# Graph network kernel: layout of the 32-bit one-hots in the bounded attention path

## The reference, cut to what matters

```python
hp = einsum('nf,hfo->hno', h, w)
e = leaky_relu(a_src[:, src] + a_dst[:, dst] + fc_b, 0.2)      # a score of each edge and head
e = exp(e - segment_max(e, src))
att = e / segment_sum(e, src)
out = mean over heads of segment_sum(att * hp[:, dst], src) + bias
```

## Time and profile before

| | |
|---|---|
| three runs | 20199.39, 20180.35, 20198.07 us; median 20198.07 us |
| profiled execution | 20195.53 us, of which its span is 20193.8 us |
| busy over the span | PE 12823.5, PEld 10964.2, DVE 14189.8, ACT 8582.0, POOL 10831.2 us |
| pairs of the attention stage | first exponent at 8914.3 us, last at 10463.8 us of the span |
| `widen_hots`, L2521 | 440 instructions, 2023 to 2157 ns each |
| mean granted TensorE clock | 0.741 of full over the span |

### The profile page before, as it was taken

One profiled execution on the slowest core, in us unless ns is written; L12 is line 12 of the kernel. 1 busy time (PEld: TensorE's weight loads), 2 busy tenths in 40 slices (PEclk: granted clock), 3 DMA queues, 4 the chain that ended last, 5 costly groups with the idle time before them and its releaser, 6 DMA issues. The chain is left out here.

```text
span 20193.8 us, 373564 instructions
## 1 busy us (share of the span) xinstructions
PE 12823.5 (64%) x81513; PEld 10964.2 (54%) x81515; DVE 14189.8 (70%) x35200; ACT 8582.0 (42%) x18845; POOL 10831.2 (54%) x11458
## 2 busy tenths in 40 slices
PE   1333333334444444459985888888878888888887
PEld 1333333334444444448873555555567777777776
DVE  5187773113222222248877999899989999999999
ACT  5611112221000000039964777577745555555554
POOL 2777777775777777741111000000037777777776
PEclk8555555555555555569987999999988888888988
DMA  2212122224322233235532333223322222222223
GB/s 65 17 16 15 15 15 17 17 17 52 69 69 68 69 69 69 69 49 49 49 34 81 102 102 102 86 102 102 103 55 43 43 43 43 43 43 43 43 43 40
DMA packets 2940092, 1096.13 MB, mean 54 GB/s; under 512 B 2414118, under 2 KB 2633479, under 8 KB 2938505
## 3 DMA queue, kind: packets, MB, share of 16 engines
q1 hardware_dynamic: 2510328, 650.25, 17.0%
q0 software_dynamic: 312576, 231.97, 7.2%
q10 hardware_dynamic: 117044, 212.38, 3.7%
HBM read 999.36 MB, written 98.48 MB: 54 GB/s over the span
## 5 line engine op out<-in xcount | busy, mean ns | idle before, releaser
L2782 POOL DMA_INDIRECT conv_far<-conv_rows x3232 | 3065.9, 949 | 2922.0 <-DMA att_far_all<-rows_by_src 2072.9
L818 POOL DMA_INDIRECT weighted_far<-in_x_dram,weighted_rows x3232 | 3338.2, 1033 | 1295.3 <-issue 984.9
L1557 POOL DMA_INDIRECT rows_by_src<-push_row,push_index x3232 | 3103.5, 960 | 1004.8 <-issue 984.9
L908 PE MATMUL weighted_total<-weighted_message,weighted_hot 128*128 128x33 f32 x6464 | 1542.9, 404 | 2817.9 <-ACT weighted_message L932 2686.4
L1334 DVE TENSOR_SCALAR hop_hots<-hop_wide_iota,hop_nodes 128x512 bf16<-128x512 f16 x11904 | 3306.2, 384 | 2.1 <-PE hop_sums_ps L1407 2.1
L2888 PE MATMUL conv_radial_a<-radial,conv_hidden 128*128 128x256 f32 x6464 | 2741.9, 512 | 637.8 <-DVE conv_products_b L3020 570.5
L1407 PE MATMUL hop_sums_ps<-hop_hots,place_i 128*96 128x512 bf16 x11904 | 2827.2, 380 | 494.3 <-DVE hop_hots L1334 376.4
L1633 PE MATMUL push_near<-far_rows_sb,push_turned 128*128 x6464 | 1682.3, 434 | 2123.4 <-DVE push_turned L1596 2122.8
L908 PEld LDWEIGHTS weighted_total<-weighted_message,weighted_hot 128*128 128x128 f32 x6464 | 1438.8, 328 | 2922.7 <-issue 2922.2
L1633 PEld LDWEIGHTS push_near<-far_rows_sb,push_turned 128*128 128x128 f32 x6464 | 1569.5, 327 | 2186.7 <-issue 2186.4
L2888 PEld LDWEIGHTS conv_radial_a<-radial,conv_hidden 128*128 128x128 f32 x6464 | 1802.8, 327 | 701.2 <-issue 636.6
(11 more groups left out here) (349 smaller groups left out, 23978.7 us busy)
## 6 DMA issues: line engine op xcount, KB each, us to landing
hop_line<-sources_of_tiles SPq DMA_DIRECT2D x744, 512.0 KB
push_line<-local_by_group ACTq DMA_DIRECT2D x808, 256.0 KB
conv_weights<-weight_by_group SPq DMA_DIRECT2D x808, 128.0 KB
att_far_all<-rows_by_src SPq DMA_DIRECT2D x880, 80.0 KB
weighted_rows<-edges_by_dst SPq DMA_DIRECT2D x3232, 4.0 KB
weighted_far<-in_x_dram,weighted_rows POOLq DMA_INDIRECT x3232, 2.4
push_place<-place_by_dst SPq DMA_DIRECT2D x3232, 0.5 KB
rows_by_src<-push_row,push_index POOLq DMA_INDIRECT x3232
```

The lines of the kernel that those rows point to most:

```text
L818: pool.indirect_dma_start(far[s][:, j, :], None, table, bass.IndirectOffsetOnAxis(ap=rows[s][:, j, 0:1].bitcast(I32), axis=0)).then_inc(ga ...
L908: last = pe.matmul(total[:].rearrange("p n c -> p (n c)")[:, bass.ds(at[s % SLOTS * HALVES + j // COLUMNS], width)], hot[b][:, j, :], mess ...
L1557: pool.indirect_dma_start(k.rows_by_src, bass.IndirectOffsetOnAxis(ap=index[s][:, j:j + 1], axis=0), row[s][:, j, :], None).then_inc(writt ...
L2782: pool.indirect_dma_start(far[s][:, j, :], None, k.conv_dram, bass.IndirectOffsetOnAxis(ap=rows[s][:, j, 0:1].bitcast(I32), axis=0)).then_ ...
```

## The change

`hot_pair(q)` keeps its place and size. A new view of it, `wide_hot(q)`, has the node outermost and the tile innermost, [128 nodes, 8 tiles], the order of `short_hot`. ACT writes through it, now reading and writing in one piece. PE takes the weights of a tile from it with a step of eight 32-bit values.

```diff
+        def wide_hot(q):
+            return hot_pair(q).rearrange("p g j n -> p (g j n)").rearrange("p (n c) -> p n c", c=2 * PER)
...
-                        last = pe.matmul(part[q % 2][:, g * HEADS * W:(g + 1) * HEADS * W], hot_pair(q)[:, g, j, :],
-                                         message_pair(q)[:, g * PER + j, :], start=(j == 0), stop=(j == PER - 1))
+                        last = pe.matmul(part[q % 2][:, g * HEADS * W:(g + 1) * HEADS * W],
+                                         wide_hot(q)[:, :, g * PER + j], message_pair(q)[:, g * PER + j, :], start=(j == 0), stop=(j == PER - 1))
...
-                act.copy(hot_pair(q).rearrange("p g j n -> p (g j) n"),
-                         short_hot[q % 2][:].rearrange("p n c -> p c n")).then_inc(p_hot_widened[q % 2], 1)
+                act.copy(wide_hot(q), short_hot[q % 2][:]).then_inc(p_hot_widened[q % 2], 1)
```

## The result

The changed kernel takes 20840.88 us (median of four runs, 20836.86 to 20841.61) against 20194.13 us for the kernel before with a fourth run counted in. The ratio is 1.0322, 95% interval 1.031 to 1.0334: slower by 647 us. The forecast was 20858 us, 1.0327.

The account below looks back on a forecast made before the run. DVE's 3.42 us, ACT's 3.3 to 3.4 and handing over made a pair 3.53 us; PE's loads would then bound it at 4.94 + 0.09 = 5.03. 440 x 1.50 = 660 us more gives 20858 us, range 20735 to 21045.

Parts of the forecast that it names:

- The widening: ACT's copy of the one-hots in attention: 1034 ns against 2117, saving 1.08 us a pair.
- The loads: PE's 16 loads a pair in `sum_nodes`: pitch 0.234 us each with the step, against 0.1125 in one piece.
- Transposes and small loads: PE's eight transposes and twenty-four small loads a pair in attention: 0.50 and 0.70 us at the full clock.
- The clock: PE in attention: 22% of the time at 1.2 GHz, as in the convolution, adding 0.09 us a pair.
- Cover: Attention stage: PE's longer pair hides DVE's turn and ACT's copies; PE's waits for DVE's messages vanish.
- The free step: Rival in `sum_nodes`: stepped loads cost PE nothing beyond 0.1125 us, DVE sets the pitch; 20150 us, 0.24% faster; chance 5%.
- The dearer step: Rival in `sum_nodes`: twice the distance costs twice the excess, 0.355 us a load; 21672 us; chance 8%.
- The low clock: Rival: clock falls for the whole attention stage, PE needs 5.33 us a pair; 20990 us; chance 10%.

Follow-up runs that it names:

- PE's half alone: Changed kernel, but ACT copies tile by tile, reading and writing with a step of eight: 652.7 us slower than the kernel before, ratio 1.0303.
- half of the columns: Changed kernel with 66 instead of 132 moving columns in `sum_nodes`, DVE adding 66 sums: 792.0 us slower than the kernel before, ratio 1.0371.
- the step of two: Against the kernel before: ACT writes runs of two values, PE loads with a step of two values (8 bytes): 48.0 us faster, ratio 0.998.

## Why the prediction was right, point by point

- *The widening*: 1034 ns estimated, 1046 measured. Right, and worth nothing here, as PE's half alone shows.
- *The loads*: the term that carries the sum. 0.234 us taken from a step of four in the convolution; measured inside the row 0.232 at a step of four and 0.237 at eight. That the price would be the same for other steps was taken from two agreeing rows; the runs bear it out within 2% between four and eight and miss it by 8% at sixteen. A row of the nearest case was good enough. The reason given for it, one price for each value that lies 16 bytes from the last, whatever the engine and type, is contradicted by a row that was at hand: the transposes' loads read 16-bit values 16 bytes apart too (of the two operands that a row names the second is the loaded one, here `short_hot`), and eight of them take 0.50 us, 0.0625 us each or 0.49 ns a value, where the 32-bit loads pay 1.83. So the agreement of TensorE's 32-bit loads with ACT's 16-bit reads is no rule. What carried the forecast is the row of the same engine and type.
- *Transposes and small loads*: 0.50 and 0.70 us taken as they were the earlier trace rows. The transposes kept 0.49. Loads and small loads together were forecast at 3.74 + 0.70 = 4.44 and take 4.51 us: 0.07 too little, since the sixteen loads cost 0.237 and not 0.234 each, the last one's end falling into the first small load. With it PE's pair is 5.00 and not 4.94.
- *The clock*: 0.09 us a pair for 22% of the time at 1.2 GHz. This step failed. But for its first 10 us the stage ran at 1.00, above the 0.98 of before, though PE's matmuls fill less of a pair. Taking the share from another stage whose loads have a step too was the mistake; that stage has idle stretches and a mix of its own. The price of the low level was right, as another run happened to show: with half of the columns the clock did stay at 0.50 and the pair was 5.33 us, the very figure of the sum. That loads with a step would keep their pitch there was right too.
- *Cover*: DVE's turn is hidden, PE waits 2.0 us for DVE's messages in the whole stage, and DVE and ACT wait for PE, as forecast.

The loads with the small ones behind them (+0.07), the transposes (-0.01) and the clock (-0.09) sum to -0.03 us a pair, 13 us of the 17 by which the forecast was too high; the fourth run of the kernel before, which lowers its median by 4 us, is the rest. An error of 40 us one way and one of 31 the other partly cancel, so that it is as close as 17 us is luck. The direction and the 3% are not: they rest on the pitch of the loads.

- *The free step* is out for a step of eight, and the step of two shows that its arithmetic was right: 48 us for DVE's pitch taking over, and a pair of 3.428 us for DVE's 3.42.
- *The dearer step* is out: doubling the distance from four to eight adds 2% and doubling again takes 8% away.
- *The low clock* did not come in this kernel, but it did with half of the columns.

The Trainium skill's "SBUF — State Buffer", section "Door 1: The DMA port swizzle", speaks of lines of 16 bytes of which two values at least must be used for full speed. The steps show just that: 0.117 us inside the row with two values to a line, 0.232 with one. That a step of sixteen costs less than one of eight (0.217 against 0.237) it doesn't say. The Trainium skill's "TensorE: Matmul & The Clock Gate", section "LDWEIGHTS (loading the stationary operand)", prices a load by its columns alone, P / 1.2 ns, which for 128 columns is an estimate of 107 ns, and names no step. For 32-bit loads that holds roughly here for steps of one and two at the 2.4 GHz level (0.1125 and 0.117 us), and for none of the larger steps.

## What to carry to other kernels

When a layout is changed to make one engine's access contiguous, look up what the other engine on that buffer pays for it, in a row that has such a step, and multiply by its count: here 1.07 us came off an engine that was not alone at the bound, and 2.0 us went onto one with 0.5 us to spare. Take the row of the same engine and the same type: TensorE's own 16-bit loads with a step of 16 bytes cost about a quarter of its 32-bit ones (0.0625 us against 0.232). A middle layout can serve both: with two 32-bit values side by side both engines keep most of their speed, and that layout is the fastest, 48 us below the kernel before. Ahead of taking an instruction out of a bounding engine's row, ask whether it fills the latency of its neighbour.

## What the runs showed of the hardware that I had not expected

- ACT pays for writes as for reads: 1024 values of 32 bits in runs of one, two and four or more cost 2041, 1157 and 1046 ns (the first with a step of 512 bytes). A slow read and a slow write in one copy cost 2120 ns, not the sum.
- A 32-bit load with a step of eight keeps its pitch at either clock level, 0.237 us inside the row with 132 moving columns, while loads in one piece go from 0.1125 to 0.216. So with 132 moving columns the step costs a tenth more at 1.2 GHz, and twice the time at 2.4 GHz.
- Less matmul work made the kernel slower: with 66 columns behind each load TensorE stayed at 1.2 GHz for the whole stage; with 132 it left that level within the stage's first two pairs and stayed at 2.4 GHz, at the same pitch of loads.
- The granted clock that a profile gives for a stretch is not always the one the engine ran at. In the weighted sum the kernel before and the changed kernel read:

```profile
1000.00:2000.00 1000.00, 338.49 (x1422) 316.05 (x1422) 769.27 (x516) 199.72 (x1050) 787.26 (x699) 0.50 0.21 16
```

```profile
1000.00:2000.00 1000.00, 338.56 (x1424) 316.46 (x1424) 769.40 (x517) 199.72 (x1050) 787.03 (x699) 1.00 0.20 16
```

The same work, PE's busy time the same to 0.1 us, and 0.50 beside 1.00. PE does nothing there but the matmuls of L908, whose 32-bit weights lie in one piece, and in both kernels their loads read, in the groups by line for the whole program:

```profile
L908 PEld LDWEIGHTS weighted_total<-weighted_message,weighted_hot 128*128 128x128 f32 x6464 | 1438.8, 328 | 2922.7 <-issue 2922.2
L908 PEld LDWEIGHTS weighted_total<-weighted_message,weighted_hot 128*128 128x128 f32 x6464 | 1438.5, 328 | 2916.8 <-issue 2916.5
```

In one piece a load lasts 192 ns at the median in the convolution, ahead of 32 columns (L908 has 33), and about 0.34 us in attention's first 11 us at 0.50. With 328 ns on the mean both kernels ran at 1.2 GHz here, and the 1.00 is wrong. In the changed kernel's trace the first record of the clock comes at 4702 us, and the profile reads 1.00 for all that lies ahead of it. So the mean over the span (0.741 before, 0.855 after) says nothing of the change; in the attention stage the small loads and transposes tell the level apart, 0.82 and 0.49 us at 1.00 against 0.91 and 0.76 at 0.50.
